# A two-layer graph kernel: GpSimd waits ahead of each gather of the second layer, not once a group

## The reference, cut to what matters

```python
Q_h = (x @ Wq + bq).reshape(N, H, D)
K_h = (x @ Wk + bk).reshape(N, H, D)
V_h = (x @ Wv + bv).reshape(N, H, D)
E = (edge_attr @ We + be).reshape(-1, H, D)
src = K_h[src_idx]
dest = Q_h[dst_idx]
score = src * dest / jnp.sqrt(jnp.asarray(D, x.dtype))
score = score * E
score = jnp.exp(jnp.clip(score.sum(-1, keepdims=True), -5.0, 5.0))
msg = V_h[src_idx] * score
wV = jax.ops.segment_sum(msg, dst_idx, num_segments=N)
Z = jax.ops.segment_sum(score, dst_idx, num_segments=N)
h_out = wV / (Z + 1e-06)
```

## Time and profile before

| | |
|---|---|
| median of 3 runs | 4904.57 us (4900.18 to 4905.06) |
| the profiled execution | 4905.26 us |
| its span, first to last instruction | 4903.4 us |
| mean granted TensorE clock | 0.649 of full speed |
| first gather of the second layer | 2405.3 us from the span's start |
| DMA over the span | 383.51 MB, mean 78 GB/s |

### The profile page before, as it was taken

The page is one execution under the profiler, slowest core; times in us unless marked ns, Lnnn a source line. Parts: engine busy times, 40 slices in busy tenths (PEclk is TensorE's granted clock), DMA queues, the critical chain, the costliest instruction groups (busy, mean ns, idle before and its releaser), DMA issues.

```text
span 4903.4 us, 43885 instructions
## 1 busy us (share of the span) xinstructions
PE 3032.8 (62%) x13152; PEld 2732.1 (56%) x13152; DVE 2272.7 (46%) x5605; ACT 869.2 (18%) x1966; POOL 3144.3 (64%) x3330
## 2 busy tenths in 40 slices
PE   3544545544555555454577777777776777677777
PEld 3443434443444444443567667667766667677776
DVE  5433444334433443344445455555555554555555
ACT  1222222222222222222201111111111111111111
POOL 6666666666666666666566666666666666666665
PEclk8666666666666666666666666665666666656665
DMA  3111111111111111111244444444444444444443
GB/s 97 40 39 41 44 39 40 44 40 39 40 44 40 40 39 45 40 39 40 70 109 114 113 113 112 110 111 116 112 112 111 114 111 112 113 113 113 113 111 95
DMA packets 290371, 383.51 MB, mean 78 GB/s; under 512 B 154382, under 2 KB 196911, under 8 KB 290127
## 3 DMA queue, kind: packets, MB, share of 16 engines
q0 software_dynamic: 132864, 251.83, 20.0%
q1 hardware_dynamic: 157263, 128.81, 9.2%
HBM read 360.62 MB, written 19.72 MB: 78 GB/s over the span
## 4 chain that ended last, share of the span: by engine, by line
another core or an unknown queue 33%; issue 26%; POOL 18%; PE 10%; DVE 7%; ACT 5%; DMA 1%; DVEq 0%; SPq 0%; ACTq 0%
POOL rows L455 18%; PE banks L537 4%; ACT onehot_t L707 3%; PE banks L595 2%; PE banks L576 2%; DVE onehot L807 2%; DMA rows<-in_x,src_i 1%; ACT banks L712 1%; PE banks L586 1%; PE banks L567 1%; DVE sums L932 1%; DVE ex L920 1%; PE banks L518 1%; DVE sums L930 0%
## 5 line engine op out<-in xcount | busy, mean ns | idle before, releaser
L455 POOL DMA_INDIRECT rows<-key_value,src_i x1661 | 1571.4, 946 | 932.5 <-issue 454.0
L455 POOL DMA_INDIRECT rows<-in_x,src_i x1661 | 1571.4, 946 | 810.0 <-issue 471.6
L537 PE MATMUL banks<-ex,onehot 128*128 128x192 f32 x3322 | 1033.0, 481 | 1007.3 <-DVE ex L920 764.8
L537 PEld LDWEIGHTS banks<-ex,onehot 128*128 128x128 f32 x3322 | 863.0, 287 | 1170.5 <-DVE ex L920 883.9
L576 PE MATMUL banks<-qw,onehot_t 128*128 128x192 f32 x1664 | 612.0, 518 | 551.4 <-ACT onehot_t L707 493.9
L576 PEld LDWEIGHTS banks<-qw,onehot_t 128*128 128x128 f32 x1664 | 443.7, 304 | 591.2 <-ACT onehot_t L707 526.2
L595 PEld LDWEIGHTS banks<-onehot,vals 128*104 128x104 f32 x3322 | 604.0, 270 | 161.3 <-issue 120.1
L595 PE MATMUL banks<-onehot,vals 128*104 128x64 f32 x3322 | 593.9, 353 | 107.9 <-issue 86.0
L567 PE MATMUL banks<-we_sb,ea 97*128 97x96 f32 x3322 | 639.9, 359 | 0.0
L567 PEld LDWEIGHTS banks<-we_sb,ea 97*128 97x128 f32 x3322 | 630.1, 282 | 0.0
L983 DVE TENSOR_TENSOR prod<-rows,banks 128x384 f32<-128x384 f32 x416 | 229.7, 552 | 826.2 <-remote 643.9
(11 more groups left out here) (107 smaller groups left out, 1524.9 us busy)
## 6 DMA issues: line engine op xcount, KB each, us to landing
ea<-in_edge_t SPq DMA_DIRECT2D x415, 192.0 KB
rows<-in_x,src_i POOLq DMA_INDIRECT x1661
rows<-key_value,src_i POOLq DMA_INDIRECT x1661
qw<-query SPq DMA_DIRECT2D x832, 24.0 KB
key_value<-qkv SPq DMA_DIRECT2D x24, 400.0 KB
x<-in_x SPq DMA_DIRECT2D x7, 672.0 KB, 9.0
query<-qkv SPq DMA_DIRECT2D x24, 192.0 KB
out<-outs SPq DMA_DIRECT2D x24, 192.0 KB
```

What stands on the lines that cost most here:

```text
L455: pool.indirect_dma_start(out=to[0:n, r, u, :], out_offset=None, in_=table, in_offset=bass.IndirectOffsetOnAxis(ap=src_i[0:n, g * G + u:g ...
L537: last = nc.tensor.matmul(ps_sum0[b], onehot[:, r, u, :], ex[:, b, u, :], start=u == 0, stop=u == n - 1)
```

## The change

In the second layer the gathers of a group are issued one at a time. For the first PACE groups nothing changes. For all others the first gather keeps its wait for `s_sum1`, the second waits for `s_tr1` at g - PACE + 3 = g (the turn of group g - 1 is done), the third for `s_ee` at g (its edge products) and the fourth for `s_qe` at g (its query product). The gathers themselves, their buffers and the first layer stay.

```diff
--- before.py
+++ after.py
@@ -449,13 +449,16 @@
             pool.iota(done_to[:, :], pattern=[[CN, NG // PER + 2], [0, PER]], base=-CN,
                       channel_multiplier=0).then_inc(s_const, 1)
 
+            def gather_tile(g, u, r, to, table, s):
+                n = TAIL_ROWS if g * G + u == ET - 1 else P
+                pool.indirect_dma_start(
+                    out=to[0:n, r, u, :], out_offset=None, in_=table,
+                    in_offset=bass.IndirectOffsetOnAxis(ap=src_i[0:n, g * G + u:g * G + u + 1], axis=0)
+                ).then_inc(s, 16)
+
             def gather(g, r, to, table, s):
                 for u in range(tiles_of_group(g)):
-                    n = TAIL_ROWS if g * G + u == ET - 1 else P
-                    pool.indirect_dma_start(
-                        out=to[0:n, r, u, :], out_offset=None, in_=table,
-                        in_offset=bass.IndirectOffsetOnAxis(ap=src_i[0:n, g * G + u:g * G + u + 1], axis=0)
-                    ).then_inc(s, 16)
+                    gather_tile(g, u, r, to, table, s)
 
             pool.wait_ge(s_src[0], 16)
             for g in range(R0):
@@ -468,9 +471,16 @@
                 for b in range(2):
                     pool.wait_ge(s_kvw[b], 16 * ((NC + 1 - b) // 2))
                 for g in range(NG):
-                    if g >= PACE:
+                    if g < PACE:
+                        gather(g, g % R1, rows, key_value, s_row1[g % R1])
+                    else:
                         pool.wait_ge(s_sum1, g - PACE + 1)
-                    gather(g, g % R1, rows, key_value, s_row1[g % R1])
+                        gather_tile(g, 0, g % R1, rows, key_value, s_row1[g % R1])
+                        marks = ((s_tr1, g - PACE + 3), (s_ee, g - PACE + 3), (s_qe, g - PACE + 3))
+                        for u in range(1, tiles_of_group(g)):
+                            s_mark, n_done = marks[u - 1]
+                            pool.wait_ge(s_mark, n_done)
+                            gather_tile(g, u, g % R1, rows, key_value, s_row1[g % R1])
                 pool.nop(nofuse=True)
 
         @block.tensor
```

## The result

The changed kernel takes **4894.27 us** (median of 15 runs, 4889.37 to 4900.59); the kernel before, run beside it, 4905.06 us (4900.18 to 4908.44, 15 runs). The ratio is 0.9977 with a 95% interval of 0.997 to 0.9984: 10.8 us faster, 0.2%, where the forecast was 4910, a little slower than before. The profiled execution took 4894.15 us with a span of 4892.4, against 4905.3 and 4903.4 before.

The account below looks back on a forecast made before the run. The prediction took PE's late marks, for which DVE and POOL wait, as the bound. 4905.3 us plus 0 to 12 (eighth gather held) and nothing for 87 late groups gave 4910; range 4885 to 4935, with rivals 4770 to 5050.

Parts of the forecast that it names:

- The state before: Second layer: POOL's eight gathers, then a 2.24 to 2.29 us wait; PE's marks up to 3.8 us behind matmul rows.
- a met wait at 0 us: Second layer's added waits, 413 x 3: a wait already met costs POOL 0 us, read at the fifth gather.
- The regular cycle's term: Second layer's two-group cycle: query mark misses its gather by 0.10 us; over about 120 pairs 12 us, or nothing.
- the value of the late marks: 87 of 413 second-layer groups with edge or query mark later than its gather: at most 139 us, taken as nothing.
- below nothing: Lower bound for the 87 second-layer groups: a gain if pausing gathers lets PE's marks out earlier; no size given.
- The forecast's sign: Second layer's POOL rows: eighth gather 0.1 us later than 8.75 us after the first, then the 2.2 us wait.
- The sign for telling the rivals apart: Gap over 0.3 us before gather 2 or 3; wait before gather 0 gone: lockstep, still about 2 us: More drains.
- lockstep: Second layer: marks come on time, PE's work bounds at 5.67 us a group; 125 us less, 4780 us; chance 0.28.
- the cover of 2 us: Second layer: gathered rows lie ready about 2 us before DVE's key product, whose 27 us wait should stay small.
- More drains: Second layer: each biting new wait costs its own 2 us drain; 5042 us, or 4934 over 87 groups; chance 0.28.
- POOL as the bound: Second layer with PE's clock at its upper level: four gathers, 5.0 us a group; 404 us less, 4501; chance 0.07.
- Nothing changed: Second layer: all added waits are met, 4905 us, the forecast's lower end; chance part of the forecast's 0.37.

Follow-up runs that it names:

- batch 1: Kernel before plus only the edge wait, and the change without its edge wait, where the kernel before takes 4193.1 us: 4192.82 and 4192.97 us, both 0.9999.
- the second chip: The changed kernel again, unedited, on another chip with late marks, beside the kernel before at 4873.8 us: 4865.23 us, 0.998.
- edge wait alone: Changed kernel with only the edge wait ahead of gather 2; waits for sums, turn and query taken out: 4853.57 us, 0.9965 of the kernel before.
- batch 3: Kernel before with one gather of four from the second layer's group 6 on, on a chip with late marks: 3926.18 us (one run).
- the query wait alone: Changed kernel with only the query wait ahead of gather 3; waits for sums, turn and edge products taken out: 4881.33 us, 1.0025 of the kernel before.
- the turn wait alone: Changed kernel with only the turn wait ahead of gather 1; waits for sums, edge products and query taken out: 4891.7 us, 1.0044 of the kernel before.

## Why the prediction was wrong

**The state before was read rightly.** POOL's cycle of eight gathers and a stop of 2.2 us, PE's marks behind its rows, and a met wait at 0 us are all borne out: the last by 0.9999 in batch 1, with no stop in the whole layer. (The added waits stand in 412 groups and not 413, which changes nothing.)

**The regular cycle's term was right in size.** 0.10 us for about 120 pairs, at most 12 us, was to be lost by the query mark held a little. Measured: holds rose from 2.1 to 5.7 us, 47 instead of 11.

**The step that failed is the value of the late marks.** The prediction counted 87 groups whose edge or query mark comes after its gather, gave bounds of +139 and "below nothing", and took nothing, with the words "the wait is moved, not added". The wait was moved: 150 of 231 stops lie at gather 2, none did before. But a moved wait isn't an equal one. Cycles of eight stop there for 1.85 us and not 1.92 (on the second chip 1.67 and 1.88), and with the stops of broken cycles counted in, the sum fell by 12.7 us. The count was low too (87 groups, against 150 stops at gather 2), for it was made with the marks where they stood before: once one stop is at gather 2, the next stream of eight also ends at gather 2, so that few late marks move many stops. The reason given for zero, that the release comes 2.0 us after the last gather in both kinds of cycle, was read from two cycles; the second chip shows 0.2 us between the places.

**The end of the kernel** had no term. It gave 2.0 us. In the kernels on late chips, from the last gather's start, it is 15 to 22 us long, with no order that I can see, so this part may belong to where the last stop happens to fall.

With what was measured in place of its terms the sum is 4905.3 + 3.6 (holds) - 12.7 (stops) - 2.0 (end) - 0.3 (first layer) = 4893.9, against 4894.15. This is the account of one trace and no proof: that it closes says only that nothing else changed. That 4894 lies within the forecast's own range of 4885 to 4935 is luck of its width, for the change went the other way.

**The signs.** The forecast's sign, the eighth gather late by 0.1 us and then the 2.2 us wait, is there in the 45 cycles of eight that stop at gather 0 at most, against 125 that stop at gather 2. The sign for telling the rivals apart failed: the wait before gather 0 is gone in most cycles, which was to mean lockstep, and a single wait of about 2 us stands before gather 2 instead, for which no rival had a sign; it was the term's "below nothing". DVE's wait for rows was to stay small and grew to 154 us, so the cover of 2 us was read too generously; it did no harm that can be seen, for the fastest kernel of the study (edge wait alone) has 173.

**The rivals.** *More drains* has its shape in the trace: after the change 31 stops follow six gathers, but they last 1.1 to 1.3 us and not 2, so that a short stream pays a short stop and this rival's price was wrong. *Lockstep* didn't come: there is no run of short waits, 47 holds in all. Its mechanism, that marks are on time where POOL pauses, is what batch 3 shows, but there the pause was most of the time (one gather in 3.66 us). Its price of 5.67 us for PE's work was no bound: with one gather the clock was granted at 0.88 and the whole group took 3.66. *POOL as the bound* is not this chip's case and is exactly the on-time chips': 5.0 us a group. *Nothing changed* is what the same change does there, as far as the two kernels of batch 1 stand for it.

The prediction took up the Trainium skill's DMA: Bandwidth & Descriptors, section SWDGE vs HWDGE vs iDMA, where POOL's transfers keep descriptor rings that POOL writes itself, as a reason why gathers might disturb others, and said that no row showed it. Batch 3 now shows the disturbance: the same marks are 0.03 us behind the row with one gather a group, and 1.9 with four. That the rings are the place of it no run shows.

**Open.** Why a stop at gathers 2 and 3 is 0.2 us shorter than at 0 and 1 is argued at most (more of the next group's work is already released when the marks come out); no run isolates it. Why some chips hold the marks back and others don't can't be told from these traces. Nor can it be told whether it is the mark itself that is late or the end of PE's work behind it, since the ends of its rows are modelled. That the regular stop goes by its place is shown by seven kernels on late chips. That the gain follows from the place isn't: the query wait alone has the short regular stop and is slower than before, and the turn wait alone has the stop of before and is slower too.

## What to carry to other kernels

Where an engine that must stop anyway has a choice of the mark at which it stops, the mark matters, by some tenths of a per cent: the edge products gave 0.9965, the query products, which need ACT first, 1.0025, and the turn, which needs no other engine's reply, 1.0044. No rule comes out of these three; each place has to be tried. Moving a stop changes all the cycles after it, so counting late marks in the old trace gives too small a number. And before such tenths are weighed, look at what the kernel before takes on the chip at hand: 4193 or 4905 us here, with other bounds in each.

## What the runs showed of the hardware

- The same program takes 4193 to 4201 us beside two of the batches and 4871 to 4908 beside the other four and the comparison. On the first, marks of PE are read 0.03 to 0.04 us behind the end of the matmul rows, with gathers back to back at 1.25 us; on the others 1.9 us behind in the median while gathers stream (edge mark, kernel before). Marks of DVE and ACT are read 0.03 to 0.06 us behind on both. The second layer begins at 2098 to 2103 us on the first and at 2389 to 2407 on the others; the first layer gathers too, and in the kernel before its gathers have no stop on the on-time chip and 122 on the late one.
- On late chips a pause of 0.08 or 0.19 us more between gathers lengthens the stretch that POOL can go without a stop: from 8 gathers to 8 or 12 (75 and 63 cycles), and to 16 or 20 (22 and 37).
- A memset of 128x1 on POOL with a wait for its end costs 0.08 us beyond the gap that is there anyway (0.384 for 0.305 us), one of 128x128 0.19, one of 128x512 0.51.
- With a memset between them, 18 gaps stand ahead of the same 18 gathers in all four runs, on the on-time chip and on the late one, most of them 96 gathers apart and 1.36 us longer than usual; what they are no run tells.
